# Gated SSM and routed low-rank FFN on one core: C of two pairs by DVE in a batch's first phase, two states by ACT's scaling and PE's turn in its last, statistics placed anew

## The reference

```python
# for each batch; DI = 512 channels, 16 states, 4 taps
xin = in_proj_w @ ctx.T                       # 512 x 512
u = silu(causal_conv4(xin) + conv_b)
dt_lo, Bm, Cm = split(x_proj_w @ u)           # 16, 16, 16 rows
delta = softplus(dt_proj_w @ dt_lo + dt_proj_b)
for t in range(L):                            # per channel and state n
    state = state * exp(delta[t] * A) + (delta[t] * u[t]) * Bm[n, t]
    y[t] = sum_n(state[n] * Cm[n, t])
y = (y + D * u) * silu(layernorm(x))
x = x + tanh(g_xattn) * y.T
h = layernorm(x)
sc = h @ Wr.T                                 # 32 experts, the best two
g = softmax(sc) * top2_mask; g = g / (sum(g) + 1e-8)
out = sum_s g[s] * (h @ U[s]) @ V[s]          # rank 16 each
x = x + tanh(g_ffn) * out * (0.9 + 0.2 * gate)
```

## Time and profile before

| what | value |
|---|---|
| median of 3 runs | 603.8 us (600.62 to 605.88) |
| the profiled execution | 602.83 us, span 601.1 us |
| PE busy | 517.5 us (86%) |
| POOL busy | 486.3 us (81%) |
| DVE busy | 468.7 us (78%) |
| ACT busy | 389.9 us (65%) |
| POOL's multiplications by C (L497) | 307.3 us in 160 |
| DVE's scans (L1083) | 320 in all, 1.21 us on 512 positions |

### The profile page before, as it was taken

The page is one execution under the profiler, slowest core; times in us unless marked ns, Lnnn a source line. Parts: engine busy times, 40 slices in busy tenths (PEclk is TensorE's granted clock), DMA queues, the critical chain, the costliest instruction groups (busy, mean ns, idle before and its releaser), DMA issues.

```text
span 601.1 us, 9365 instructions
## 1 busy us (share of the span) xinstructions
PE 517.5 (86%) x3162; PEld 393.7 (65%) x3162; DVE 468.7 (78%) x839; ACT 389.9 (65%) x678; POOL 486.3 (81%) x365
## 2 busy tenths in 40 slices
PE   6659689798876899999969999999599998999686
PEld 2147669667756696769658778677566775766452
DVE  3558789878885999789977999798578878688640
ACT  3366495858754778477846877578389777777421
POOL 0089689969998999879999999789889998688700
PEclk9768799999987999999999999999799999799969
DMA  3196000007420001045120000155000000000000
GB/s 86 50 359 260 2 1 1 36 6 233 152 71 1 1 1 53 0 157 218 54 70 2 19 2 18 52 216 193 1 18 19 2 19 18 16 5 18 19 1 35
DMA packets 17986, 37.29 MB, mean 62 GB/s; under 512 B 5505, under 2 KB 6017, under 8 KB 17938
## 3 DMA queue, kind: packets, MB, share of 16 engines
q1 hardware_dynamic: 17938, 36.69, 17.5%
HBM read 32.23 MB, written 4.46 MB: 61 GB/s over the span
## 4 chain that ended last, share of the span: by engine, by line
PE 48%; POOL 26%; ACT 10%; issue 10%; DVE 5%; DMA 1%; DVEq 0%; POOLq 0%; SPq 0%; ACTq 0%
PE p_s L664 14%; POOL state L497 12%; PE p_y L683 10%; POOL dbu L484 6%; PE p_v L715 4%; PE p_tr L635 4%; PE p_f L706 3%; POOL pair_b L460 3%; DVE state L1083 3%; PE p_pr L599 3%; ACT da L867 2%; POOL du L471 2%; ACT L835 1%; PE p_f L696 1%; ACT p_s L867 1%
## 5 line engine op out<-in xcount | busy, mean ns | idle before, releaser
L497 POOL TENSOR_TENSOR state<-state,c_bc 128x1024 f32<-128x1024 f32 (+1 forms) x160 | 307.3, 1925 | 47.3 <-DVE state L1083 44.3
L1083 DVE TENSOR_TENSOR_SCAN state<-da,p_s 128x512 f32<-128x512 f32 (+1 forms) x160 | 175.6, 1106 | 46.4 <-PE p_s L664 42.3
L664 PEld LDWEIGHTS p_s<-pair_b,du_t 128*128 128x128 f32 x1280 | 170.5, 201 | 37.1 <-issue 25.1
L664 PE MATMUL p_s<-pair_b,du_t 128*128 128x128 f32 x1280 | 184.5, 287 | 6.0 <-ACT du_t L841 4.8
L683 PE MATMUL p_y<-ident,state 128*128 128x128 f32 x1024 | 152.4, 278 | 0.5 <-POOL state L497 0.5
L867 ACT ACTIVATE da<-delta,a_neg 128x512 f32<-128x512 f32 (+1 forms) x192 | 119.7, 642 | 29.1 <-DVE state L1083 29.0
L683 PEld LDWEIGHTS p_y<-ident,state 128*128 128x128 f32 x1024 | 122.4, 144 | 20.8 <-issue 18.3
L484 POOL TENSOR_TENSOR dbu<-du,pair_b 128x1024 f32<-128x1024 f32 (+1 forms) x64 | 116.2, 1815 | 0.1
L867 ACT ACTIVATE p_s<-delta,a_neg 128x512 f32<-128x512 f32 (+1 forms) x128 | 73.7, 582 | 43.6 <-DVE state L1083 42.8
L1083 DVE TENSOR_TENSOR_SCAN state<-p_s,dbu 128x512 f32<-128x512 f32 (+1 forms) x96 | 98.7, 1034 | 0.0
L706 PE MATMUL p_f<-u_sb,h_t 128*128 128x512 f32 x112 | 55.1, 594 | 1.3 <-DVE gw L1171 1.3
(11 more groups left out here) (169 smaller groups left out, 629.1 us busy)
## 6 DMA issues: line engine op xcount, KB each, us to landing
c_bc<-bc_rows SPq DMA_DIRECT2D x32, 512.0 KB, 5.5
pair_b<-bc_rows SPq DMA_DIRECT2D x12, 512.0 KB, 5.3
...
```

Of the source, the lines that this page charges most:

```text
L497: eng.tensor_tensor(pair, pair, c_bc[:, 2 * p:2 * p + 2, c0:c0 + w], ALU.mult).then_inc(po_cs, 1)
L664: mm = eng.matmul(p_s[g % BANKS][:, t * P:(t + 1) * P], du_t[:, f % 2, t, :], diagonals_of(n // 2)[:, n % 2, c0 // P + t, :], start=(t == ...
L1083: eng.tensor_tensor_scan(slot(g)[:, 0:w], decayed, added, first, ALU.mult, ALU.add).then_inc(ve_scan, 1)
```

## The change

Six things, each in the diff below, cut to its core.

- In phases 0, 4 and 8, C of pairs 1 and 4 is multiplied by DVE, after the scans of states 4 and 10 (`C_BY_DVE`, DVE's new `times_c`); POOL leaves these two out, and waits and counts follow (`c_by_pool`, `c_by_dve`).
- In phases 3, 7 and 11, states 14 and 15 (pair 7) are no longer du_t times a diagonal. ACT multiplies the four blocks of `du_t` by B as a scale for each partition and writes them over the diagonals of pair 7, two blocks after each of the decays 0, 2, 4 and 6 (`scale_du`); PE turns them into the same bank.
- `scale_of_z` for batch b + 1 moves on POOL from phase 4, 8, 12 to the phase before, and its result has two places. The z statistics follow: `Z_STATS` has two in phases 1, 5 and 9, one in the two phases after each, and none in 4, 8 and 12.
- `STATS` goes: row tile T has its statistics in phase T + 4, at steps 0 to 2, or at steps 10 and 11 in phases 4, 8, 12 and 16. `scale_of_f` stands behind pair 3's C, or behind pair 5's in those four phases.
- On ACT, `tanh_v` stands ahead of `normed` at step 15.
- `copy_b` also waits for the scalings before it.

```diff
...
+ACT_PAIR = 7
 POOL_SETS = [[2, 5], [2, 4, 6], [2, 4, 6], [1, 3, 5, 7]]
...
     def pe_pairs(b):
...
+    def scaled_phase(f):
+        b, k = PHASE[f][:2]
+        return k == Q - 1 and b + 1 < B
...
     def on_pool(f, n):
...
     POOL_TILES = [(f, p) for f in range(F) for p in pool_pairs(PHASE[f][0])]
+    SCALED = [(f, n, t) for f in range(F) if scaled_phase(f) for n in (2 * ACT_PAIR, 2 * ACT_PAIR + 1)
+              for t in range(Q)]
     DIAGONALS = [(b, p) for b in range(B) for p in pe_pairs(b)]
...
-    STATS = {}
-    for T in range(EARLY):
-        STATS.setdefault(rows_ready(T) + (0, 0, 1, 2)[T % Q] if rows_ready(T) < F else rows_ready(T), []).append(T)
+    C_BY_DVE = [(Q * b, p) for b in range(B - 1) for p in (1, 4)]
+    C_BY_POOL = [(f, p) for f in range(F) for p in range(PAIRS) if (f, p) not in C_BY_DVE]
+    c_by_dve = {pair: i for i, pair in enumerate(C_BY_DVE)}
+    c_by_pool = {pair: i for i, pair in enumerate(C_BY_POOL)}
...
+    Z_STATS = {}
+    for q in range(Q, BLOCKS):
+        Z_STATS.setdefault(q - Q + (1, 0, 0, 0)[q % Q], []).append(q)
...
         zv = sb("zv", [P, 2, Q])
-        zr = sb("zr", [P, 4, Q])
+        zr = sb("zr", [P, 2, 4, Q])
         zh = sb("zh", [P, L])
...
         ac_da = sem("act_decay")
+        ac_scale = sem("act_du_times_b")
         ac_z = sem("act_z")
...
         ve_scan = sem("dve_scanned")
+        ve_cs = sem("dve_c_times_state")
         ve_sz = sem("dve_silu_z")
...
             def broadcast_c(b, p):
                 if b:
-                    eng.wait_ge(po_cs, PAIRS * (Q * b - 1) + p + 1)
+                    eng.wait_ge(po_cs, c_by_pool[first_phase(b) - 1, p] + 1)
                 broadcast(b, NS + 2 * p, c_bc[:, 2 * p:2 * p + 2, :]).then_inc(s_cbc[p], 16)
             def store_out(T):
...
             def times_c(f, p):
                 b, k, c0, w = PHASE[f]
+                if (f, p) in c_by_dve:
+                    return
                 g = NS * f + 2 * p
...
             def scale_of_z(b):
                 eng.wait_ge(ve_zs, 2 * Q * (b + 1))
-                if b:
-                    eng.wait_ge(ac_z, 2 * Q * b)
+                if b >= 2:
+                    eng.wait_ge(ac_z, 2 * Q * (b - 1))
                 eng.tensor_tensor(zv[:, 0, :], zmv[:, :, 1], eps_c[:, :], ALU.add).then_inc(po_zs, 1)
...
                 eng.wait_ge(po_zs, ZOPS * b + 2)
-                eng.tensor_tensor(zr[:, 0, :], zv[:, 1, :], half[:, :], ALU.mult).then_inc(po_zs, 1)
+                eng.tensor_tensor(zr[:, b % 2, 0, :], zv[:, 1, :], half[:, :], ALU.mult).then_inc(po_zs, 1)
                 eng.tensor_tensor(zv[:, 0, :], zv[:, 1, :], minus_half[:, :], ALU.mult).then_inc(po_zs, 1)
                 eng.wait_ge(po_zs, ZOPS * b + 4)
-                eng.tensor_tensor(zr[:, 1, :], zmv[:, :, 0], zv[:, 0, :], ALU.mult).then_inc(po_zs, 1)
+                eng.tensor_tensor(zr[:, b % 2, 1, :], zmv[:, :, 0], zv[:, 0, :], ALU.mult).then_inc(po_zs, 1)
                 eng.wait_ge(po_zs, ZOPS * b + 5)
                 eng.wait_ge(ac_k, 2)
-                eng.tensor_scalar(zr[:, 2:4, :], zr[:, 0:2, :], gx[:, :], None, ALU.mult).then_inc(po_zs, 1)
+                eng.tensor_scalar(zr[:, b % 2, 2:4, :], zr[:, b % 2, 0:2, :], gx[:, :], None, ALU.mult).then_inc(po_zs, 1)
             def scale_of_f(T):
...
                     times_b(f, pairs[-1])
-                if k == 0 and c0 == 0 and b:
-                    scale_of_z(b)
                 times_c(f, 3)
+                if Q <= f < EARLY + Q and f % Q:
+                    scale_of_f(f - Q)
                 if many:
...
                     times_b(f + 1, pool_pairs(PHASE[f + 1][0])[0])
-                if STATS.get(f):
-                    scale_of_f(STATS[f][0])
+                if Q <= f < EARLY + Q and f % Q == 0:
+                    scale_of_f(f - Q)
                 if turning:
+                    scale_of_z(b + 1)
                     diagonals(b + 1, 1)
...
                 times_c(f, 7)
-                for T in STATS.get(f, [])[1:]:
-                    scale_of_f(T)
             for T in range(EARLY, TILES):
...
                     eng.wait_ge(ac_turn, TURN["du", f] + 1)
-                if k == 0 and c0 == 0 and n % 2 == 0:
+                scaled = scaled_phase(f) and n // 2 == ACT_PAIR
+                if scaled:
+                    eng.wait_ge(ac_scale, SCALED.index((f, n, Q - 1)) + 1)
+                elif k == 0 and c0 == 0 and n % 2 == 0:
                     eng.wait_ge(po_diag, DIAGONALS.index((b, n // 2)) + 1)
...
                 for t in range(w // P):
-                    mm = eng.matmul(p_s[g % BANKS][:, t * P:(t + 1) * P], du_t[:, f % 2, t, :], diagonals_of(n // 2)[:, n % 2, c0 // P + t, :],
-                                    start=(t == 0), stop=(t == w // P - 1))
+                    to = p_s[g % BANKS][:, t * P:(t + 1) * P]
+                    by_b = diagonals_of(n // 2)[:, n % 2, c0 // P + t, :]
+                    if scaled:
+                        mm = eng.matmul(to, by_b, ident[:, :], is_transpose=True, start=(t == 0), stop=(t == w // P - 1))
+                    else:
+                        mm = eng.matmul(to, du_t[:, f % 2, t, :], by_b, start=(t == 0), stop=(t == w // P - 1))
                 mm.then_inc(pe_dbu, 1)
             def skip(f):
...
             def add_y(f, n):
-                eng.wait_ge(po_cs, PAIRS * f + n // 2 + 1)
+                if (f, n // 2) in c_by_dve:
+                    eng.wait_ge(ve_cs, c_by_dve[f, n // 2] + 1)
+                else:
+                    eng.wait_ge(po_cs, c_by_pool[f, n // 2] + 1)
                 blocks = PHASE[f][3] // P
...
             def copy_b(b):
                 if b:
+                    eng.wait_ge(ac_scale, sum(PHASE[f][0] < b for f, n, t in SCALED))
                     eng.wait_ge(po_diag, DIAGONALS.index((b, pe_pairs(b)[0])))
...
                 copy_turn("du", f, du_t[:, f % 2, 0:PHASE[f][3] // P, :])
...
+            def scale_du(f, n, blocks):
+                eng.wait_ge(ac_turn, TURN["du", f] + 1)
+                eng.wait_ge(pe_dbu, by_pe[f - 1, n] + 1)
+                for t in blocks:
+                    eng.activation(diagonals_of(n // 2)[:, n % 2, t, :], du_t[:, f % 2, t, :], ACT.Copy,
+                                   scale=b_t[:, n, t:t + 1]).then_inc(ac_scale, 1)
             def decay(f, n):
...
                         eng.wait_ge(pe_turn, TURN["sz", f - 1] + 1)
-                    eng.activation(zh[:, 0:w], source, ACT.Identity, bias=zr[:, 3, k:k + 1],
-                                   scale=zr[:, 2, k:k + 1]).then_inc(ac_z, 1)
+                    eng.activation(zh[:, 0:w], source, ACT.Identity, bias=zr[:, b % 2, 3, k:k + 1],
+                                   scale=zr[:, b % 2, 2, k:k + 1]).then_inc(ac_z, 1)
                 else:
...
                         eng.wait_ge(ac_out, f - 5)
-                    eng.activation(p_v[:, 0:w], source, ACT.Tanh, bias=zr[:, 1, k:k + 1],
-                                   scale=zr[:, 0, k:k + 1]).then_inc(ac_z, 1)
+                    eng.activation(p_v[:, 0:w], source, ACT.Tanh, bias=zr[:, b % 2, 1, k:k + 1],
+                                   scale=zr[:, b % 2, 0, k:k + 1]).then_inc(ac_z, 1)
             def copy_sz(f):
...
                 if T == EARLY:
-                    eng.wait_ge(po_cs, PAIRS * F)
+                    eng.wait_ge(po_cs, len(C_BY_POOL))
                 eng.activation(h_of(T), x2_of(T), ACT.Identity, bias=fr[:, T % Q, 1:2],
...
                     decay(f, n)
+                    if scaled_phase(f) and n in (0, 2, 4, 6):
+                        scale_du(f, 2 * ACT_PAIR + n // 4, ([0, 1], [2, 3])[n // 2 % 2])
                     if f == 0 and n == 1:
...
                             copy_du(f + 1)
+                        if f + 5 < BLOCKS:
+                            tanh_v(f + 5)
                         if Q <= f < EARLY + Q:
                             normed(f - Q)
-                        if f + 5 < BLOCKS:
-                            tanh_v(f + 5)
...
                 eng.tensor_tensor_scan(slot(g)[:, 0:w], decayed, added, first, ALU.mult, ALU.add).then_inc(ve_scan, 1)
...
+            def times_c(f, p):
+                b, k, c0, w = PHASE[f]
+                g = NS * f + 2 * p
+                eng.wait_ge(ve_scan, g + 2)
+                eng.wait_ge(s_cbc[p], 16 * (b + 1))
+                pair = state[:, g % RING:g % RING + 2, 0:w]
+                eng.tensor_tensor(pair, pair, c_bc[:, 2 * p:2 * p + 2, c0:c0 + w], ALU.mult).then_inc(ve_cs, 1)
             def silu_z(f):
...
                         eng.wait_ge(ve_k, 6)
-                    if n == 1 and 1 <= f and f + 3 < BLOCKS:
-                        z_statistics(f + 3)
+                    if n == 1:
+                        for q in Z_STATS.get(f, []):
+                            z_statistics(q)
+                    if n % 2 == 0 and (f, n // 2 - 1) in c_by_dve:
+                        times_c(f, n // 2 - 1)
                     if n == 2 and mid >= 0:
```

(27 more changed lines are left out.)

## The result

The kernel with the change takes 608.59 us (median of four runs, 608.08 to 610.25); the kernel before, run beside it on the same chip, 602.26 (600.62 to 605.88). The ratio is 1.0087, with a 95% interval of 1.005 to 1.0124: slower by 0.9%, 5.2 us by the ratio. (Ratios and intervals leave out runs that are over 1.5% above the fastest of the same kernel.) The forecast was 601.4 us, a small gain. The time lies inside its range, by 0.4 us; the direction is the other one.

The account below looks back on a forecast made before the run. POOL was taken to set phases 4 and 8, its late fr stalling DVE; both engines nearly set the others. Against 602.8 us, +1.2 - 2.4 - 2.1 + 0.8 - 0.4 + 1.6 - 0.1 = -1.4 gave 601.4 us, range 594 to 609.

Parts of the forecast that it names:

- the cost of the moved statistics: Phases 5 and 9: z statistics moved onto DVE, which has little slack, cost +0.4 us each, bounds 0 and 0.8.
- The second term: Phases 3, 7 and 11: ACT's scalings delay xd, score exponent and softplus, +1.6 us in all, bounds 0 and 7.2.
- the 2 us that the prediction named as a sign of being wrong: Phases 3, 7 and 11: growth by over 2 us would show the forecast wrong on the slower side.
- rival 1: C's on DVE share memory with POOL at no price on either side: 596.8 us, chance 0.25.
- rival 2: Phases 4 and 8: each C on DVE waits for a whole POOL operation, 2.36 us: 606.6 us, chance 0.09.
- The gain of phases 4 and 8: C's moved to DVE let POOL's fr come earlier, shortening the end-of-phase stall: -2.4 and -2.1 us.
- 4.3 us a phase: Phases 4 and 8: the waits of the C's on DVE beyond which DVE's port waiting decides the outcome.
- Rival 4: Phases 4 and 8 win 0: POOL is held as long as it saves, fr comes unchanged: 605.9 us, chance 0.10.
- Rival 3: Phases 3, 7 and 11: ACT's scalings all show, 7.2 us in place of 1.6: 607.0 us, chance 0.09.
- Scale of z: Moving it on POOL to the phase before wins nothing; later B arrives before DVE; phase 12 keeps its end: 0.
- Phase 0: C of pair 1 on DVE falls in idle time, 0; C of pair 4 costs +1.2 us, bounds 0 and 2.4.
- the forecast of -0.4: Phases 16 and 17 together, from row statistics moved between them on DVE: -0.4 us, bounds -1.5 and 0.8.

Follow-up runs that it names:

- experiment 1: Changed kernel with the gates' one-element DVE operation reading one tensor input in SBUF, its second operand a pointer scalar: 600.58 us, ratio 0.995 to the kernel before.
- 3: Changed kernel with all C's back on POOL, the rest of the change kept: 612.05 us, ratio 1.0131 to the kernel before.
- 6: Changed kernel with neither C's on DVE nor ACT's scalings, leaving moved statistics, z's scale and tanh's place: 607.98 us, ratio 1.0077 to the kernel before.
- experiment 5: Kernel before with only the C's of pairs 1 and 4 in phases 0, 4 and 8 on DVE: 597.08 us, ratio 0.9895.
- 13: Changed kernel with all C's on POOL, no scalings, and the gates' operation on one tensor input: 603.22 us, ratio 0.9988 to the kernel before.
- 11: Changed kernel with all row statistics at steps 10 and 11 and scale_of_f behind pair 5's C: 618.12 us, ratio 1.0263 to the kernel before.
- 4: Changed kernel without ACT's scalings, states 14 and 15 by POOL's diagonals as before: 603.79 us, ratio 1.0012 to the kernel before.
- 7: Changed kernel with the gates' operation on one tensor input and without ACT's scalings: 596.44 us, ratio 0.9899 to the kernel before.
- Experiment 10: Kernel before with C's on DVE in phases 4 and 8 alone and the gates' operation on one tensor input: 590.66 us, ratio 0.9805.
- 9: Kernel before with C's on DVE in phases 0, 4 and 8 and the gates' operation on one tensor input: 593.99 us, ratio 0.9862.
- experiment 8: Changed kernel with the gates' operation on one tensor input, no scalings, and phase 0's C's back on POOL: 598.39 us, ratio 0.991 to the kernel before.

## Why the prediction was wrong

**The step that failed** is the cost of the moved statistics: "Phases 5 and 9 have little slack (2.1 of 29.40): +0.4 each, bounds 0 and 0.8." I priced them as DVE's busy time against its slack. Phase 5 grew by 2.77 us and phase 9 by 1.07. The cause is shown from four sides: with the operation on one input, phase 5 falls by 2.75 us and phase 9 by 2.0 (experiment 1); the collision stays when the C's go back to POOL (3) and when the scalings go too (6); it is not there with the C's alone, where 1.11 us are left of it (5); and with one input the statistics cost nothing that shows (13). I had the pieces: the earlier trace rows was my evidence for the port, and the prediction even used the 2.28 us as a price for the new C's. I did not ask it of the operation that it was a row of. The operation has that price wherever it stands, and what decides its size is where POOL's starts fall. A move that puts 1.6 us more on DVE ahead of it changes those places, so the bound of 0.8 on each side was no bound: one full POOL instruction (2.36 us) less what it paid before belonged to it, for each such operation downstream. That term alone is 2.0 us for phase 5 and 2.1 for phase 9, whose growth is smaller because the relief takes 1.1 off that phase (29.05 for 30.18 in experiment 5).

With the operation on one input in both kernels, the change stands 0.2% under the kernel before (0.995 and 0.9971, intervals that overlap), which is the small gain of the forecast. That the rest of the sum comes out so near is luck in part: the scalings cost more than forecast, and the relief gave more. The measured time's place inside the range is no merit of the sum either, since the upper end was put there for the dearer rivals.

**The second term** is the scalings: +1.6 forecast, 3.1 to 4.5 measured in company of the statistics. Their own instructions came out as priced (0.39 and 0.34 us), and PE's wait for xd and DVE's for the exponent grew as argued. By the profiles phases 3, 7 and 11 carry 2.3 us of it, of which 1.4 are the V matmuls of phase 7 at the lower clock. Those matmuls take 3.15 to 3.54 us in the four kernels that have both the scalings and the moved statistics (the change, 1, 3 and 11), and 1.88 in the twelve others, those with the scalings alone too. Why it takes both is not shown. The forecast gave the clock no part. Phase 7's growth of 2.38 us passes the 2 us that the prediction named as a sign of being wrong; phases 3 and 11 grew by 0.36 and 1.02. The other 1 to 2 us are not placed: the profiles differ as well in phase 0 and in the start, where executions of the same code differ.

**What held.** The C's beside POOL: 1.22 us with POOL idle, 1.5 to 2.8 with POOL busy, and POOL's next 0.8 to 1.0 longer. So rival 1 (no price) is out, and rival 2 (each waits a whole instruction) too: their waits in phases 4 and 8 were 0.3, 1.5, 1.6 and 0.9. The gain of phases 4 and 8: -2.4 and -2.1 forecast, -3.45 and -1.48 measured, -4.5 against -4.9 in sum. In phase 4 the first scans of the next phase no longer stand behind PE's backlog (the wait of 1.70 us in the earlier trace rows is gone); in phase 8 DVE, not fr, comes last, as was said. The prediction's own terms put that point lower than its "4.3 us a phase": DVE decides once the waits pass 5.1 - 0.75 - 2.1 = 2.25 us in phase 8, and they were 2.5; at 4.35 the phase would have won nothing. The relief is a gain of 1.05% by itself (experiment 5), and of 0.4 to 0.9% in company (3 against the change, 6 against 4, 13 against 7). Rival 4 is refuted by the same.

**Rival 3** (all of the scalings show, 607.0 us) comes out near the time measured, but for half of the reason: they cost 3 to 4.5 us and not 7.2, and the statistics' collision makes up the rest. Rival 2 (606.6 us) had the right mechanism at the wrong operation. And "no change of under 1% can be told from noise" was too pessimistic: the interval of the result is 0.37% to either side, enough to tell a loss of 0.9% from the small gain forecast.

**Scale of z.** POOL's stretch in phase 12 keeps its end, but DVE now waits 2.5 us there for dbu, with the scale ahead of it on POOL; I had said that B would come "before DVE is there". The phase grew by 0.4 us, so it was nearly free all the same. The line of the wait, kernel after:

```profile
423.70 0.69 DVE L1120 TENSOR_TENSOR_SCAN state<-p_s,dbu 128x256 f32<-128x256 f32 x1 [2.51 <-POOL dbu L500]
```

**Phase 0** was forecast at +1.2 and came at +2.75, with the start 1.1 later. In it the C of pair 4 took a plain 1.21 us on DVE, and C of pair 1 stood in an idle time, as said. The rest is PE: its projection for delta took 2.04 us (46.90, kernel after) where it took 1.09 (45.24, kernel before), and DVE waits behind it:

```profile
45.24 1.09 PE L610 MATMUL p_pr<-xd,w_dt 17*128 17x512 f32 x2 [3.32 <-DVE u L1042]
46.90 2.04 PE L627 MATMUL p_pr<-xd,w_dt 17*128 17x512 f32 x2 [3.32 <-DVE u L1079]
50.98 1.22 DVE L1120 TENSOR_TENSOR_SCAN state<-da,p_s 128x512 f32<-128x512 f32 x1 [1.96 <-PE p_s L689]
```

But among the kernels with the C's on POOL in phase 0 this phase takes 32.6 to 35.2 us, and among those with them on DVE 34.1 to 35.7: the stretch at the lower clock falls in or not. Like against like, the profiles say what the C's cost. Where this projection takes 1.1 to 1.3 us, the phase is 32.6 to 32.9 us with the C's on POOL (six kernels) and 34.1 to 34.5 with them on DVE (four), so some 1.5 us. Where it takes 2.04, it is 34.9 to 35.2 (three) and 35.5 to 35.7 (three), so some 0.6. The forecast's +1.2 lies between; what it lacked is the slow projection, 1.3 to 2.2 us, which is there with the C's on either engine and of which nothing here shows the cause. In whole times this is less clear. Experiment 10 against 9 (590.66 and 593.99, intervals that overlap) points to some, experiment 8 against 7 to none. Phases 13 and 17, 2.5 us shorter in sum, differ in the same way between kernels that are alike there, and I count them neither for nor against the forecast of -0.4.
